# A decoder kernel on Trainium2: level weights of stage 1 made by three bf16 products in place of one fp32 product

## The reference, cut to what matters

```python
lam = softplus(dl + Lparam)                      # (b, t, head, level)
G = cumsum(-softplus(x @ Wg.T + bg), axis=1)
scores = einsum('bthd,bshd->bhts', q, k) * scale
decay = exp(where(mask, Gh[t] - Gh[s], -inf))
lamw = einsum('bthl,tsl->bhts', lam, one_hot(level(t - s)))
A = scores * decay * lamw
y = einsum('bhts,bshd->bthd', A, v)
```

## Time and profile before

| what | us |
|---|---|
| median of 3 runs | 1442.98 |
| the profiled execution | 1450.22 |
| its span, first to last instruction | 1448.4 |
| busy: PE, PEld | 1359.2, 1051.9 |
| busy: DVE, ACT, POOL | 917.2, 809.5, 658.9 |
| mean granted TensorE clock | 0.981 of full speed |

### The profile page before, as it was taken

The page is one execution under the profiler, slowest core; times in us unless marked ns, Lnnn a source line. Parts: engine busy times, 40 slices in busy tenths (PEclk is TensorE's granted clock), DMA queues, the critical chain, the costliest instruction groups (busy, mean ns, idle before and its releaser), DMA issues.

```text
span 1448.4 us, 38328 instructions
## 1 busy us (share of the span) xinstructions
PE 1359.2 (94%) x14549; PEld 1051.9 (73%) x14549; DVE 917.2 (63%) x2416; ACT 809.5 (56%) x1590; POOL 658.9 (45%) x664
## 2 busy tenths in 40 slices
PE   6999999988999989999789998899999999998997
PEld 4776777767777767887566666778888888875864
DVE  5555555547887864434788887676667766766123
ACT  4555555546787764545477886755555555542521
POOL 3454555444245632016778776633334444443044
PEclk9999999998998999999899999999999999999999
DMA  5021230000756702247000000000000000001323
GB/s 138 20 67 45 68 119 8 13 1 31 276 204 233 269 23 82 81 137 264 22 10 2 2 2 2 15 2 6 6 6 8 12 12 8 9 13 50 116 57 89
DMA packets 97085, 91.56 MB, mean 63 GB/s; under 512 B 21645, under 2 KB 71434, under 8 KB 96650
## 3 DMA queue, kind: packets, MB, share of 16 engines
q1 hardware_dynamic: 92298, 79.66, 17.0%
q0 software_dynamic: 4608, 9.45, 2.1%
HBM read 30.87 MB, written 58.21 MB: 62 GB/s over the span
## 4 chain that ended last, share of the span: by engine, by line
PE 63%; POOL 10%; issue 10%; DVE 7%; ACT 6%; DMA 2%; SPq 1%; POOLq 0%; DVEq 0%; ACTq 0%
PE bank L3308 6%; PE bank L1711 5%; PE bank L3343 5%; PE bank L1695 5%; PE bank L3322 5%; PE bank L3296 4%; PE bank L2681 3%; PE bank L2691 2%; POOL s_p L1346 2%; PE bank L3334 2%; PE bank L998 2%; PE bank L954 2%; PE bank L924 2%; PE bank L1684 2%; PE bank L975 2%
## 5 line engine op out<-in xcount | busy, mean ns | idle before, releaser
L3080 POOL TENSOR_TENSOR s_p<-s_p,s_inverse 128x616 f32<-128x616 f32 x64 | 77.0, 1223 | 200.6 <-DVE s_inverse L3223 200.6
L1459 ACT COPY s_pT<-bank 77x512 f32<-77x512 f32 (+1 forms) x256 | 135.2, 585 | 44.9 <-PE bank L1695 44.7
L1695 PE MATMUL bank<-ident,s_p 128*77 128x128 f32 (+1 forms) x1024 | 141.9, 286 | 10.7 <-ACT s_p L1450 7.7
L1695 PEld LDWEIGHTS bank<-ident,s_p 128*77 128x77 f32 (+1 forms) x1024 | 118.0, 150 | 36.0 <-issue 17.0
L1346 POOL TENSOR_TENSOR s_p<-s_p,s_peak 128x1024 f32<-128x1024 f32 x64 | 121.1, 1898 | 29.9 <-DVE s_peak L1562 29.8
L1450 ACT ACTIVATE s_p<-s_p 128x616 f32<-128x616 f32 (+1 forms) x128 | 110.7, 885 | 24.1 <-POOL s_p L1346 20.1
L3207 DVE TENSOR_REDUCE s_peak<-bank 128x8 f32<-128x616 f32 x64 | 50.7, 792 | 92.3 <-PE bank L3322 92.3
L3138 ACT ACTIVATE s_p<-s_p 128x616 f32<-128x616 f32 x64 | 46.9, 733 | 81.7 <-DVE s_p L3211 81.7
L3308 PE MATMUL bank<-pos_bias,s_ctx 128*32 128x128 f32 x3072 | 90.5, 274 | 1.7 <-ACT s_kT L3118 1.7
L1711 PE MATMUL bank<-s_pT,s_v 77*32 77x128 f32 (+1 forms) x2048 | 72.0, 282 | 18.6 <-DVE x_all L1596 18.0
L1548 DVE TENSOR_TENSOR s_p<-bank,pos_bias 128x1024 f32<-128x1024 f32 x64 | 77.7, 1215 | 18.0 <-PE bank L1684 18.0
(11 more groups left out here) (374 smaller groups left out, 3375.5 us busy)
## 6 DMA issues: line engine op xcount, KB each, us to landing
sorted_tokens<-s_zero SPq DMA_DIRECT2D x4, 5632.0 KB, 19.7
sorted_tokens<-s_zero SPq DMA_DIRECT2D x8, 2560.0 KB, 16.1
routed_tokens<-s_routed SPq DMA_DIRECT2D x24, 256.0 KB, 2.4
s_tokens<-sorted_tokens SPq DMA_DIRECT2D x48, 64.0 KB, 1.8
s_rows<-sorted_tokens SPq DMA_DIRECT2D x48, 64.0 KB, 1.8
x_all<-x SPq DMA_DIRECT2D x8, 256.0 KB, 3.3
w_s_gateup<-s_gateup SPq DMA_DIRECT2D x1, 2048.0 KB
out<-x_all SPq DMA_DIRECT2D x8, 256.0 KB, 2.6
```

Source lines behind the costliest of these rows:

```text
L1459: nc.scalar.copy(pT[0:keys, b % 2, 4 * q:4 * q + 4, :].rearrange("m h t -> m (h t)"), bank[0:keys, flip_bank("p", b, q), :]).then_inc(drai ...
L1695: last = nc.tensor.transpose(bank[0:keys, into, j * T:(j + 1) * T], p[:, b % 2, 4 * q + j, :], core.ident[:, :])
L3080: nc.gpsimd.tensor_tensor(part, part, inverse[:, b % 2, heads].unsqueeze(2).to_broadcast([P, HU, M]), ALU.mult).then_inc(share_ready, 1)
```

## The change

Each number of `lam` is written as a sum of three bf16 numbers: its rounding to bf16, the rounding of what is left, and the rest. The product with the 0/1 band is then three bf16 matmuls that add up in PSUM, in place of one fp32 matmul. What it does, part by part:

- DVE: `lam_parts_of(g)` in step 4g-1, four operations of 128 x 256 on `lam` (cast, subtract, cast, subtract), the last writes the third part. Then `last_level_of(step + 1)` in every step, just ahead of `aT_of`: one 128 x 1024 product of the third part with `own`.
- POOL: `level_of` issues two 128 x 1024 products, for the first and the second part, and waits for the third operation of `lam_parts_of` where it waited for the landed `lam`.
- PE: three bf16 matmuls where one fp32 matmul stood, with a bf16 copy of `band` that DVE makes once, in step -3; it waits for POOL's two products and for DVE's one.
- `lam` has one buffer. The loads for group g wait for the parts of group g - 1 to be made, in place of the level weights of group g - 2.
- DVE writes the weight over the decay, so `decay_of(u)` on ACT waits for `aT_of(u - 2)` in place of `weight_of(u - 2)`, and `weight_of` has one wait less.
- `z` is written over `y`: `z_of` no longer waits for the x of the group before, and `y_of` waits for the x of two groups before in place of its z. `next_part` is written over `first_part`.

```diff
-        lam = sbuf("s1_lam", [P, 2, NB, G, H1])
-        level = sbuf("s1_level", [P, 2, NB, H1, TB])
+        lam = sbuf("s1_lam", [P, NB, G, H1])
+        lam_parts = sbuf("s1_lam_parts", [P, 2, 3, NB, G, H1], BF16)
+        level = sbuf("s1_level", [P, 2, 3, NB, H1, TB], BF16)
+        band = sbuf("s1_band", [P, 2 * T - TB], BF16)
...
-                if g >= 2:
-                    sp.wait_ge(level_ready, G * (g - 1))
+                if g:
+                    sp.wait_ge(lam_parts_ready, 4 * g)
...
             def level_of(b):
                 g, n = b // G, b % G
-                pool.wait_ge(lam_landed, (g + 1) * 16 * LEVELS)
+                pool.wait_ge(lam_parts_ready, 4 * g + 3)
                 if b >= 2:
                     pool.wait_ge(level_done, max(early_of(b - 2), late_of(b - 2)) + 1)
-                nc.gpsimd.tensor_tensor(
-                    level[:, b % 2, :, :, :],
-                    lam[:, g % 2, :, n, :].unsqueeze(3).to_broadcast([P, NB, H1, TB]),
-                    w.own[:, :].unsqueeze(1).unsqueeze(1).to_broadcast([P, NB, H1, TB]),
-                    ALU.mult).then_inc(level_ready, 1)
+                for part in range(2):
+                    nc.gpsimd.tensor_tensor(
+                        level[:, b % 2, part, :, :, :],
+                        lam_parts[:, g % 2, part, :, n, :].unsqueeze(3).to_broadcast([P, NB, H1, TB]),
+                        w.own[:, :].unsqueeze(1).unsqueeze(1).to_broadcast([P, NB, H1, TB]),
+                        ALU.mult).then_inc(level_ready, 1)
...
             def decay_of(u):
                 act.wait_ge(filled, place["decay", u] + 1)
                 if u >= 2:
-                    act.wait_ge(weight_ready, u - 1)
+                    act.wait_ge(aT_ready, u - 1)
...
+            def lam_parts_of(g):
+                dve.wait_ge(lam_landed, (g + 1) * 16 * LEVELS)
+                if g >= 2:
+                    dve.wait_ge(level_ready, 2 * G * (g - 1))
+                    dve.wait_ge(last_level_ready, G * (g - 1))
+                nc.vector.tensor_copy(lam_parts[:, g % 2, 0, :, :, :], lam[:, :, :, :]).then_inc(lam_parts_ready, 1)
+                dve.wait_ge(lam_parts_ready, 4 * g + 1)
+                nc.vector.tensor_tensor(lam[:, :, :, :], lam[:, :, :, :], lam_parts[:, g % 2, 0, :, :, :],
+                                        ALU.subtract).then_inc(lam_parts_ready, 1)
+                dve.wait_ge(lam_parts_ready, 4 * g + 2)
+                nc.vector.tensor_copy(lam_parts[:, g % 2, 1, :, :, :], lam[:, :, :, :]).then_inc(lam_parts_ready, 1)
+                dve.wait_ge(lam_parts_ready, 4 * g + 3)
+                nc.vector.tensor_tensor(lam_parts[:, g % 2, 2, :, :, :], lam[:, :, :, :],
+                                        lam_parts[:, g % 2, 1, :, :, :], ALU.subtract).then_inc(lam_parts_ready, 1)
+
+            def last_level_of(b):
+                g, n = b // G, b % G
+                dve.wait_ge(lam_parts_ready, 4 * g + 4)
+                if b >= 2:
+                    dve.wait_ge(level_done, max(early_of(b - 2), late_of(b - 2)) + 1)
+                nc.vector.tensor_tensor(
+                    level[:, b % 2, 2, :, :, :],
+                    lam_parts[:, g % 2, 2, :, n, :].unsqueeze(3).to_broadcast([P, NB, H1, TB]),
+                    w.own[:, :].unsqueeze(1).unsqueeze(1).to_broadcast([P, NB, H1, TB]),
+                    ALU.mult).then_inc(last_level_ready, 1)
+
             def weight_of(u):
                 dve.wait_ge(decay_ready, u + 1)
                 dve.wait_ge(level_done, u + 1)
-                if u >= 2:
-                    dve.wait_ge(aT_ready, u - 1)
-                nc.vector.tensor_tensor(weight[:, u % 2, :], decay[:, u % 2, :], bank[:, LEVEL + u % 2, :],
+                nc.vector.tensor_tensor(decay[:, u % 2, :], decay[:, u % 2, :], bank[:, LEVEL + u % 2, :],
                                         ALU.mult).then_inc(weight_ready, 1)
...
                 if b // G >= 2:
-                    dve.wait_ge(z_ready, b // G - 1)
+                    dve.wait_ge(x_ready, b // G - 1)
...
                 dve.wait_ge(rstd2_ready, g + 1)
-                if g:
-                    dve.wait_ge(x_ready, g)
...
                 if step == SOFT:
                     for h in range(H1):
                         fold_keep(h)
+                    dve.wait_ge(w.landed["s1"], w.count["s1"])
+                    nc.vector.tensor_copy(band[:, :], w.band[:, :]).then_inc(band_ready, 1)
+                if group_at(step, -1) is not None:
+                    lam_parts_of(group_at(step, -1))
+                if 0 <= step + 1 < BATCH:
+                    last_level_of(step + 1)
                 if 0 <= step < BATCH:
                     for u in units_of(step):
                         aT_of(u)
...
-                return nc.tensor.matmul(
-                    bank[rows, LEVEL + u % 2, c * H1 * TB:(c + 1) * H1 * TB],
-                    w.band[:, start:start + rows.stop - rows.start],
-                    level[:, b % 2, a, :, :].rearrange("p h b -> p (h b)"), start=True, stop=True, **position)
+                for part in range(3):
+                    last = nc.tensor.matmul(
+                        bank[rows, LEVEL + u % 2, c * H1 * TB:(c + 1) * H1 * TB],
+                        band[:, start:start + rows.stop - rows.start],
+                        level[:, b % 2, part, a, :, :].rearrange("p h b -> p (h b)"), start=(part == 0),
+                        stop=(part == 2), **position)
+                return last
 
             def level_of(u):
                 b = batch_of(u)
-                pe.wait_ge(level_ready, b + 1)
+                pe.wait_ge(band_ready, 1)
+                pe.wait_ge(level_ready, 2 * (b + 1))
+                pe.wait_ge(last_level_ready, b + 1)
```

More of the change, by code:

```diff
@@ L332, in stage1 @@
         decay = sbuf("s1_decay", [P, 2, HALF])
-        weight = sbuf("s1_weight", [P, 2, HALF])
         aT = sbuf("s1_aT", [P, 2, H1, T])
@@ L545, in add_to_x @@
                 x = core.x[:, g * G:(g + 1) * G, :]
[L546 removed]
+                nc.gpsimd.tensor_tensor(x, x, z, ALU.add).then_inc(x_ready, 1)
             nc.gpsimd.memset(core.minus_half[:, :], -0.5)
@@ L795, in product @@
                     bank[rows, SCORE + u % 2, :].rearrange("p (a h b) -> p a h b", h=H1, b=TB),
-                    weight[rows, u % 2, :].rearrange("p (a h b) -> p a h b", h=H1, b=TB), ALU.mult)
+                    decay[rows, u % 2, :].rearrange("p (a h b) -> p a h b", h=H1, b=TB), ALU.mult)
             def aT_of(u):
@@ L833, in z_of @@
                 dve.wait_ge(rstd2_ready, g + 1)
-                if g:
-                    dve.wait_ge(x_ready, g)
                 for n in range(G):
-                    last = nc.vector.tensor_scalar(z[:, n, :], y[:, g % 2, n, :], moments2[:, n, 0:1], rstd2[:, n:n + 1],
+                    last = nc.vector.tensor_scalar(y[:, g % 2, n, :], y[:, g % 2, n, :], moments2[:, n, 0:1], rstd2[:, n:n + 1],
                                                    ALU.subtract, ALU.mult)
```

17 lines of the change are left out of this document (9 added, 8 removed).

## The result

The changed kernel takes **1485.49 us** (median of 4 runs, 1479.81 to 1488.06), beside 1443.0 us before (median of 4 as well): 1.0287 times as long, 95% interval 1.0265 to 1.0309. Its profiled execution took 1484.8 us, with a span of 1482.5 and a mean granted clock of 0.976.

A forecast was written before the change was run, and what follows sets the result against it. PE was taken to bound stage 1. Terms 17.1 (4g) + 16.1 (4g+2) + 2.8 (4g+3) + 5.2 (start) - 3.6 (twelve other steps) = 37.6 us gave 1487.8 for the profiled execution, 1481 for the median; range 1453 to 1510.

The forecast's parts named there:

- the two places: Chain y, moments, rstd, level product in steps 0, 4, ... 20; DVE's full order around columns_of_keys in step 14.
- Price on PE: Three bf16 matmuls for one fp32: late unit costs 0.66 us, saves 0.3; early unit taken as nothing; 9.6 us in 32 steps.
- Step 4g: Steps 0, 4, ... 20: POOL's pair behind rstd, then DVE's product, hold PE; +2.85 us each, 17.1 for six.
- Step 4g+2: Seven steps 2, 6, ... 26: DVE's product behind columns_of_keys and add_to_x's first part holds PE; +2.3 us each, 16.1 in all.
- Step 4g+3: Seven steps 3, 7, ... 27: lam operations, POOL's pair, DVE's product one behind the other; +0.4 us each, 2.8 in all.
- The start: Before PE's first levels: band copy, lam operations, POOL's pair and DVE's product; +5.2 us, side by side +3.5.
- Rival 3: TensorE clock falls to 1.2 GHz after PE's wait in each of six steps 4g, 2 us each; 1493 us, chance 0.10.
- Costed at nothing: Single lam buffer, y_of's wait, decay's wait for aT: no cost; weights up to 1 us later if DVE's product were early.
- Rival 1: POOL's and DVE's products run side by side everywhere; 1458 us, chance 0.12.
- rival 2: DVE loses the memory to every POOL series of products; 1500 to 1520 us, chance 0.15.
- Rival 4: Not slower: bf16 products cost POOL and DVE half; +2 to +10 us, 1445 to 1453, chance 0.10.
- Rival 5: Faster: all 9.6 us saved on PE, 9.6 more in early units, POOL's waits gone; chance 0.03.

The follow-up runs named there:

- e1: Changed kernel with POOL making the level weights (level_of) ahead of rstd_of; 1469.36 us, 1.0173 times the kernel before.
- e2: Changed kernel with DVE making the lam parts and its third product ahead of y, moments and columns_of_keys; 1469.91 us, 1.0172 times the kernel before.
- e4: Changed kernel with 14 overwritten fp32 matmuls keeping PE busy ahead of the level weights in steps 4g+1; 1478.06 us, 1.0230 times the kernel before.
- e6: Changed kernel with own copied once into PSUM, so DVE's third product reads one operand there; 1467.89 us, 1.0166 times the kernel before.
- e5: Kernel before with only the weight written over the decay and z over y, fp32 level weights kept; 1442.27 us, 0.9997 times the kernel before.
- e3: Changed kernel with the edits of e1 and e2 together; 1458.10 us, 1.0091 times the kernel before.
- e8: e3 with lam_parts_of ahead of weight_of and add_to_x one step later; 1447.13 us, 1.0021 times the kernel before.
- e7: Changed kernel without the third part, DVE's product and PE's third matmul, fourth lam operation cut to one number; 1443.91 us, 1.0011 times the kernel before.
- e9: e8 and e6 together, with DVE's product placed behind y_of; 1439.59 us, 0.9987 times the kernel before.
- e11: Kernel before with only the POOL order of e1 (level_of ahead of rstd_of); 1441.24 us, 0.9985 times the kernel before.

## Why the prediction was right, and where not

The total stands: 1481 us were predicted and 1485.49 measured, and the two places that were to decide did. But some terms were off in opposite directions.

- **PE's bound and the two places.** Right. The waits for POOL and DVE add up to 23.4 + 14.4 = 37.8 us, "some 35" were said. Removing one (e1) gives back 9.7 of the 15.8 us in 4g, removing the other (e2) 12.0 of the 12.8 in 4g+2.
- **Price on PE.** The late unit takes 0.67 us, predicted 0.66. Early and late together take 1.48, so the early one takes 0.81 where I took 1.0, the middle of 0.66 and 1.3. Steps 28 and 29, without waits, last 7.43 and 8.89 us against 7.78 and 9.38: PE saves 0.35 in an even step and 0.49 in an odd one, 0.3 were taken for both. The Trainium skill (TensorE: Matmul & The Clock Gate, Back-to-back issue gap) gives 81 ns for a load and a matmul of 128 columns; here it is 0.67 us for 12, 56 ns. The trace does not agree with that figure for twelve in a row. The prediction also weighed a rule of the same page of the Trainium skill (Weight-path perf modes), that the fast load needs 128 weights. The price drawn from it, an early unit 0.3 us dearer, did not come: it got 0.2 cheaper. Whether the 64-column loads took the fast path no run here shows.
- **Step 4g.** The size is near (an undisturbed step grew from 8.14 to 10.63, +2.5, against +2.85), the account is wrong in one sentence: "DVE does not get in between two products issued back to back". It does, in the fence of steps 16 to 17: the product starts 0.04 us after the first POOL product, ends 2.95 later, and the second POOL product runs to 211.29. So POOL ends last, not DVE. Since the two share one way in turn, the sum is 4.76 us either way, close to the 5.1 taken. The sentence was read from `shift_of`, and of that operation it held again, in step 1 (below).
- **Step 4g+2.** The mechanism is as told, in the first gap of `add_to_x`; one typical step grew from 8.22 to 10.57, +2.35 (predicted +2.3). The seven came to 12.8 us in place of 16.1, because not all of them were undisturbed before: step 10, for one, took 9.14 us there and 10.57 after.
- **Step 4g+3.** +0.4 per step was predicted. With no drop of the clock a step went from 10.23 to 9.98, so the pair was hidden ("side by side") and PE's saving stayed.
- **Step 1.** This is a term that was wrong in the sum: it was among the twelve steps that save 0.3 us, and it grew by 3.3. The prediction had read in the earlier trace rows that `shift_of` is held to the end of POOL's products, and did not ask what two more of them would do to it.
- **The start.** +3.7 us, near the bound of +3.5; POOL's pair ended last (27.08 to 32.07), with DVE in between as in 4g:

```profile
27.08 4.99 POOL L513 TENSOR_TENSOR s_level<-s_lam_parts,w_own 128x1024 bf16<-128x1024 bf16 x2 [1.48 <-DVE s_lam_parts L800]
...
27.50 2.81 DVE L810 TENSOR_TENSOR s_level<-s_lam_parts,w_own 128x1024 bf16<-128x1024 bf16 x1
...
32.17 1.44 PE L989 MATMUL bank<-s_level,s_band 128*128 128x128 bf16 x12 [5.17 <-POOL s_level L513]
```

- **The clock.** This is the other term that was missing from the sum. Rival 3 had it, at 2 us for each of six waits, with a chance of 0.10. It came true in part: three of the five waits of 4g from step 4 on were followed by a slow step, and two steps 4g+3 were slow behind the wait in 4g+2. e4 shows 5.8 us of it in steps 5, 13 and 21 by taking it away; steps 7 and 15 add 1.31 + 1.57 = 2.9, read off the step lengths and not removed alone. Some 9 us of the 39.5 are the clock. The argument against it ("the wait is shorter than that one") was no reason: waits of 3.14 us were enough at times, and in e6 2.16.
- **Costed at nothing.** Right for the buffers as such (e5), and right in the condition: "if DVE's product were early, the cover would go". e3 is that case. I had put up to 1 us on it. In e3 the late parts of `lam` kept POOL waiting for 1.02 us in step 15; together with `add_to_x` ahead of the pair they cost 1.6 us in each step 4g+3 (80.00 in e3 less 68.87 in e8, by 7), and no run separates the two.
- **Rivals 1, 2, 4 and 5.** The products do not run side by side while both operands lie in SBUF; bf16 is no cheaper on POOL (1938 ns in e6, 1934 for fp32 before); rival 2 came true in step 1 alone, where DVE lost to all four POOL products; in 4g and 4g+2 it got its turn after one.

With the clock taken out, stage 1 would have grown by some 31 us, 7 less than forecast (an estimate from the terms above). So that the total came out within 5 us is in part luck: four terms were too high, by 10 us together (4g+2 by 3.3 us, the start by 1.5, 4g by 1.3, 4g+3 by 4.1 once 2.9 of the clock are taken off it), and the clock (9) and step 1 (3.6 above its term) filled the gap. The two places that carry most of the loss, and the waits in them, were forecast by their mechanism, and e1, e2, e6 and e7 bear them out. What stays open: why the clock falls behind some waits of equal length and not behind others, why DVE gets a turn between POOL's products in one place and not in another, and the 9 us by which the later, unchanged stages scatter.

## What to carry to other kernels

Before work is moved from the bounding engine to one with idle time, look at the chain that ends just before each use, not at the busy share: here PE's real saving of 0.35 to 0.5 us a step was paid for with stalls of 2.4 us in two steps of four. With an order that gives the new work room, and one operand in PSUM, the stalls vanish, but what is left of the gain (e9: ratio 0.9987, interval up to 1.0005) is not told apart from none, and 2.3 of its 5.9 us in stage 1 come with the POOL order alone (e11). When a stall is removed, ask at once which chain it had been covering.
